# Attention probabilities transposed by DMA instead of by TensorE, with the exponentials left in PSUM

## What is computed

```
x = x + layernorm(attn(layernorm(x)))
x = x + layernorm(ffn(layernorm(x)))

attn(h): q, k, v = h@Wq, h@Wk, h@Wv          # rotary embedding on q and k
         p = softmax(where(causal, q@k^T, -1e9) / sqrt(64))
         return (p@v) @ Wo
ffn(h):  h @ weight^T + bias + lora(h)        # an adapter of rank 16 picked per batch
```

## Time and profile before

| | |
|---|---|
| Median of 3 runs | 2261.73 us |
| The profiled execution's own time | 2262.72 us |
| Its span, first to last instruction | 2260.9 us |
| PE busy | 2151.5 us, 95% of the span |
| DVE, ACT, POOL busy | 61%, 35%, 34% |
| Granted TensorE clock, mean | 0.978 |
| First slot of phase 1 starts, phase 2 starts | 98.44 us, 1516.18 us |

### The profile page before, as it was taken

The page is one execution under the profiler, slowest core; times in us unless marked ns, Lnnn a source line. Parts: engine busy times, 40 slices in busy tenths (PEclk is TensorE's granted clock), DMA queues, the critical chain, the costliest instruction groups (busy, mean ns, idle before and its releaser), DMA issues.

```text
span 2260.9 us, 35372 instructions
## 1 busy us (share of the span) xinstructions
PE 2151.5 (95%) x12928; PEld 1104.9 (49%) x12928; DVE 1386.0 (61%) x3295; ACT 791.6 (35%) x1797; POOL 773.7 (34%) x905
## 2 busy tenths in 40 slices
PE   3979999999999999999999998779999999999997
PEld 1445555555555555555555554444444444444443
DVE  6776566676576576566567565675555555555554
ACT  4544444444344444444444443532111111111111
POOL 0245455464554545455454544520000000000000
PEclk8999999999999999999999999979999999999999
DMA  7000010010010010010001020041433333423232
GB/s 294 1 29 15 20 43 11 24 34 19 24 31 24 10 43 24 10 44 20 15 29 33 15 85 10 20 177 47 121 94 84 97 82 97 117 64 114 62 79 56
DMA packets 98772, 125.47 MB, mean 55 GB/s; under 512 B 71745, under 2 KB 71745, under 8 KB 97570
## 3 DMA queue, kind: packets, MB, share of 16 engines
q1 hardware_dynamic: 98594, 123.12, 18.0%
HBM read 72.77 MB, written 33.55 MB: 47 GB/s over the span
## 4 chain that ended last, share of the span: by engine, by line
PE 90%; DVE 5%; issue 2%; POOL 1%; DMA 1%; ACT 1%; SPq 0%; POOLq 0%; DVEq 0%; ACTq 0%
PE ps L568 29%; PE ps L435 10%; PE ps L436 9%; PE ps L437 9%; PE ps L469 6%; PE ps L460 5%; PE ps L446 5%; PE ps L448 5%; PE ps L447 5%; PE ps L480 5%; PE ps L590 1%; PE ps L425 1%; POOL arena L1131 1%; DVE arena L711 1%; DVE w_part L620 1%
## 5 line engine op out<-in xcount | busy, mean ns | idle before, releaser
L1131 POOL TENSOR_TENSOR arena<-arena,row_inv 128x512 f32<-128x512 f32 (+3 forms) x512 | 357.9, 735 | 651.2 <-DVE row_inv L722 651.2
L435 PE MATMUL ps<-arena,region 128*128 128x512 f16 x1024 | 389.5, 380 | 0.0
L436 PE MATMUL ps<-arena,region 128*128 128x512 f16 x1024 | 388.9, 380 | 0.0
L437 PE MATMUL ps<-arena,region 128*128 128x512 f16 x1024 | 388.5, 379 | 0.0
L568 PE MATMUL ps<-region 128*128 128x512 f16 x1536 | 341.2, 383 | 8.5 <-ACT arena L1083 4.6
L807 DVE CUSTOM_DVE_ANT_0 arena<-ps,con,pow 128x512 f32<-128x512 f32 (+3 forms) x512 | 246.5, 547 | 162.1 <-PE ps L460 161.9
L568 PE MATMUL ps<-region,arena 128*128 128x512 f16 x1536 | 337.3, 379 | 0.0
L1050 ACT ACTIVATE arena<-arena,neg_max 128x512 f32<-128x512 f32 (+3 forms) x512 | 280.0, 548 | 99.3 <-DVE neg_max L807 99.3
L698 DVE TENSOR_TENSOR rotated<-ps,con 128x512 f32<-128x512 f32 x128 | 88.5, 691 | 266.7 <-PE ps L437 266.7
L568 PEld LDWEIGHTS ps<-region 128*128 128x128 f16 x1536 | 151.2, 99 | 193.5 <-issue 10.3
L1083 ACT ACTIVATE arena<-ps,sm 128x1024 f32<-128x1024 f32 x64 | 77.0, 1204 | 477.2 <-DVE sm L883 477.2
(11 more groups left out here) (121 smaller groups left out, 2668.2 us busy)
## 6 DMA issues: line engine op xcount, KB each, us to landing
arena<-x SPq DMA_DIRECT2D x32, 512.0 KB, 3.8
attn_scratch<-o_st SPq DMA_DIRECT2D x64, 256.0 KB, 2.2
region<-attn_scratch SPq DMA_DIRECT2D x8, 2048.0 KB, 8.8
v_split<-x SPq DMA_DIRECT2D x32, 512.0 KB, 4.2
out<-v_split SPq DMA_DIRECT2D x32, 512.0 KB, 5.1
arena<-wv SPq DMA_DIRECT2D x4, 1024.0 KB, 13.6
region<-wq SPq DMA_DIRECT2D x4, 1024.0 KB, 18.6
arena<-wk SPq DMA_DIRECT2D x4, 1024.0 KB, 5.5
```

The source lines that it names most:

```text
L435: mm(o, w[:, k, 0, cols], xnt[par][:, k, 0, :], start=(k == 0), stop=False)
L436: mm(o, w[:, k, 0, cols], xnt[par][:, k, 1, :], start=False, stop=False)
L437: last = mm(o, w[:, k, 1, cols], xnt[par][:, k, 0, :], start=False, stop=(k == KT - 1))
L1131: gp.tensor_tensor(unit_sb(j, a), unit_sb(j, a), row_inv[:, n:n + 1].broadcast_to([PART, 128 * (j + 1)]), ALU.mult).then_inc(norm_done, 1)
```

## The change

The scores stay in PSUM: DVE masks them in place and ACT takes the exponential in place. DVE takes all eight reciprocals at once and multiplies them by 2^14. ACT then writes the high part of the normalised probabilities (PSUM to SBUF, float16, scaled by a per-row factor) and DVE the low part, both as rows by query into `p_split`; POOL's `normalise` is gone. SP issues one transposing DMA of `p_split` (both parts, both heads: 128x5120 float16, 40 blocks of 128x128) into `pt`, after the low parts of the slot are done and the p@v products of the slot, which read the pair before from `pt`, are done. PE's `p_transposes` go. The p@v products read blocks of `pt` in 36 matmuls instead of 24, with the same number of columns, into bank 6, and wait for the DMA and for the first four low parts of the slot. Blocks of queries are now taken in the order 2, 0, 3, 1.

The normalised x of the next batch is split into two float16 tiles (ACT `xn_high_part`, DVE `xn_low_part`) and transposed by two DMAs of 128x1024, for batches 1 to 7; PE's `x_transposes` stay for batch 0 only. x comes in tile by tile into one buffer, each after the tile before is split.

As `p_split` and the x tile use the space in which Wo and Wf were staged, these come through two 1 MB buffers, and two chunks of each are loaded a second time for the split; two chunks of Wf after the last transposing DMA. `part_max` of Wo moves from slots 0 and 1 of the last batch to 1 and 2.

The diff, cut to its core:

```diff
-Q_ORDER = (3, 2, 0, 1)
-S_OFF = {3: 0, 2: 512, 0: 896, 1: 1024}
+Q_ORDER = (2, 0, 3, 1)
+S_OFF = {2: 0, 0: 384, 3: 512, 1: 1024}
 S_LEN = 1280
-UNITS = [(j, a) for j in Q_ORDER for a in range(2)]
+NB = S_LEN // PART
+UNITS = [(2, 0), (0, 0), (2, 1), (0, 1), (3, 0), (3, 1), (1, 0), (1, 1)]
 ...
+READY = (2, 2, 4, 4, 5, 6, 7, 8)
 ...
+PV_PIECES = {0: ((0, 2), (2, 2)), 1: ((1, 1), (2, 2)), 2: ((2, 2),), 3: ((3, 1),)}
+
+BANK_O = 6
 ...
+        raw_late = [arena2[:, at:at + 2048].rearrange("p (k n) -> p k n", k=KC) for at in (4096, 6144, 0, 2048)]
 ...
+
+        x_tile = arena2[:, 0:1024]
+        xn_high_t = arena2[:, 1024:1536].bitcast(F16)
 ...
-        scores = arena1[:, 4096:4096 + 2 * S_LEN].rearrange("p (a n) -> p a n", a=2)
-        pt = half(arena1[:, 6656:6656 + 2 * S_LEN], ("p (h g q) -> p h g q", dict(h=2, g=NG)))
+        pt = half(arena1[:, 6656:6656 + 2 * S_LEN], ("p (h n q) -> p h n q", dict(h=2, n=2 * NB)))
+        p_split = half(arena2[:, 1536:1536 + 2 * S_LEN], ("p (h a n) -> p h a n", dict(h=2, a=2)))
 ...
+                if not last_b and 1 <= p <= ST:
+                    tok = slice(128 * (p - 1), 128 * p)
+                    for hl, src in enumerate((xn_high_t, xn_low_t[:, :])):
+                        sp.wait_ge(xn_split[hl], n)
+                        if p == 1 and hl == 0 and not first:
+                            sp.wait_ge(qk_done[1], PAIRS * b)
+                        sp.nop(nofuse=True)
+                        sp.dma_start_transpose(xnt[1 - bp][:, :, hl, tok], src).then_inc(xnt_in[hl], 16)
                 if not last_b and p < ST:
 ...
+                    if first and p == 0:
+                        sp.wait_ge(xt_done, 2 * ST)
+                    else:
+                        need(sp, xn_split[1], n)
+                    sp.dma_start(x_tile, x_v[b + 1, p]).then_inc(x_next_in, 16)
+                if not (first and p == 0):
+                    sp.wait_ge(pv_done, g)
+                sp.wait_ge(p_done[1], 8 * g + 8)
+                sp.nop(nofuse=True)
+                sp.dma_start_transpose(pt[:, :, :, :].rearrange("p h n q -> p (h n) q"),
+                                       p_split[:, :, :, :].rearrange("p h a n -> p (h a n)")).then_inc(pt_in[0], 16)
 ...
+                if last_b and p == 0:
+
+                    for c in (0, 1):
+                        load_raw(W_O, c)
+                if last_b and p in (1, 6):
+                    w = {1: W_O, 6: W_F}[p]
+                    for c in (2, 3):
+
+                        sp.wait_ge(part_max_done, CHUNKS * {W_O: 1, W_F: 2}[w] + c - 1)
+                        load_raw(w, c)
+                if last_b and p == 4:
+                    for n in (0, 1):
+
+                        sp.wait_ge(w_low_done, CHUNKS * W_O + n + 1)
+                        load_raw(W_O, n, again=True)
+                if last_b and p == 5:
+                    for n in (0, 1):
+
+                        sp.wait_ge(w_low_done, CHUNKS * W_O + n + 3)
+                        load_raw(W_F, n)
+                if last_b and p == PAIRS - 1:
+                    phase2_loads()
 ...
+            sp.wait_ge(pt_in[0], 16 * PAIRS * B)
+            for c in (0, 1):
+                load_raw(W_F, c, again=True)
 ...
-            def p_transposes():
-                for bank, blocks in PT_GROUPS:
-                    for n, (a, kt, j) in enumerate(blocks):
-                        at = S_OFF[j] + 128 * kt
-                        last = nc.tensor.transpose(ps[:, bank, 128 * n:128 * n + 128], scores[:, a, at:at + 128],
-                                                   ident)
-                    last.then_inc(pt_done, 1)
-
 ...
-                        for a in range(2):
-                            grp, c = PT_ROW[kt][a]
-                            last = mm(ps[64 * a:64 * a + 64, BANK_O, 128 * kt:S],
-                                      v_split[:, kt, 2 * pair + a, HD * vl:HD * vl + HD], pt[:, hl, grp, c:c + n],
-                                      start=(kt == 0 and hl == 0 and vl == 0), stop=(kt == ST - 1 and hl == 1))
+                        for j, nq in PV_PIECES[kt]:
+                            at = S_OFF[j] // 128 + kt
+                            step = (S_OFF[j + 1] - S_OFF[j]) // 128 if nq == 2 else 1
+                            for a in range(2):
+                                blocks = pt[:, hl, NB * a + at:NB * a + at + (nq - 1) * step + 1:step, :]
+                                last = mm(ps[64 * a:64 * a + 64, BANK_O, 128 * j:128 * (j + nq)],
+                                          v_split[:, kt, 2 * pair + a, HD * vl:HD * vl + HD], blocks,
+                                          start=(kt == 0 and hl == 0 and vl == 0 and j == 0), stop=(kt == ST - 1 and hl == 1))
 ...
-                need(pe, pt_low, NG * g)
+                need(pe, p_done[1], 8 * g)
 ...
-                need(pe, masked, 8 * g + 8)
-                if not last_b and 1 <= p <= ST:
-                    need(pe, xn_done, 4 * b + 4 + p)
-                    for hh in range(2):
-                        x_transposes(p - 1, hh, BANK_XT[hh])
-                if has_qk:
                     need(pe, v_low, v_before(kind, p, b))
                     qk_product(1, n_pair, n_bp, range(KT), 1 - bank)
                 if not (first and p == 0):
+                    need(pe, p_done[1], 8 * g + 4)
                     need(pe, v_low, v_before(kind, p, b))
+                    need(pe, pt_in[0], 16 * g)
                     pv_products((p - 1) % PAIRS)
-                need(pe, norm_done, 8 * g + 8)
-                if not last_b and 1 <= p <= ST:
-                    need(pe, xt_low, 8 * b + 8 + 2 * p)
-                p_transposes()
                 if v_slot(kind, p):
 ...
-            def pt_evac(grp, n):
-
-                need(dve, pt_high, NG * n + grp + 1)
-                v.scalar_tensor_tensor(pt[:, 1, grp, :], ps[:, PT_GROUPS[grp][0], :], P_UP, pt[:, 0, grp, :],
-                                       ALU.mult, ALU.subtract).then_inc(pt_low, 1)
+            def p_low_part(g, n):
+
+                j, a = UNITS[n]
+                need(dve, p_done[0], 8 * g + READY[n])
+                v.scalar_tensor_tensor(unit_p(j, a, 1), unit_ps(j, a), row_inv[:, n:n + 1], unit_p(j, a, 0),
+                                       ALU.mult, ALU.subtract).then_inc(p_done[1], 1)
 ...
-            def inverse(g, part):
-
-                need(dve, exp_done, 8 * g + 4 * part + 4)
-                v.reciprocal(row_inv[:, 4 * part:4 * part + 4], row_sum[:, 4 * part:4 * part + 4]).then_inc(inv_done, 1)
+            def inverse(g):
+
+                need(dve, exp_done, 8 * g + 8)
+                v.reciprocal(row_rec[:, :], row_sum[:, :]).then_inc(recip_done, 1)
+                need(dve, recip_done, g + 1)
+                v.tensor_scalar(row_inv[:, :], row_rec[:, :], P_UP, None, ALU.mult).then_inc(inv_done, 1)
 ...
-                    if n in (0, 2, 6):
-                        need(dve, s_done, 3 * g + {0: 1, 2: 2, 6: 3}[n])
-                    if n == 0:
-                        need(dve, pt_done, NG * g)
+                    if n in (0, 4, 6):
+                        need(dve, s_done, 3 * g + {0: 1, 4: 2, 6: 3}[n])
                     v.nop(nofuse=True)
-                    v.tensor_tensor_reduce(out=unit_sb(j, a), in0=unit_ps(j, a), in1=causal[:, 512 - width:512],
+                    v.tensor_tensor_reduce(out=unit_ps(j, a), in0=unit_ps(j, a), in1=causal[:, 512 - width:512],
                                            scale=pow2[:, S_NEG:S_NEG + 1], scalar=HIGHEST, op0=ALU.add, op1=ALU.min,
                                            accum_out=neg_max[:, n:n + 1]).then_inc(masked, 1)
                 q = (p - 1) % PAIRS
                 if v_slot(kind if p > 0 else kind - 1, q) and not (first and p == 0):
 
                     v_evac(q % 4, 1 if q < 4 else 0, v_before(kind, p, b) - 1, 1 - bank)
-                inverse(g, 0)
+                if not last_b and 1 <= p <= ST:
+                    xn_low_part(4 * b + p - 1)
+                inverse(g)
                 if has_qk:
                     qk_drain(0, g + 1, bank)
-                inverse(g, 1)
-                if not last_b and p < ST:
-                    need(dve, x_in[p], 16 * (b + 2))
-                    ln_stats(p, 4 * b + 4 + p)
-                if not last_b and 1 <= p <= ST:
-                    for hh in range(2):
-                        xt_evac(p - 1, hh, 1 - bp, 8 * b + 8 + 2 * (p - 1) + hh, BANK_XT[hh])
-                if last_b and p < 2:
-                    part_max(W_O, 2 * p)
-                    part_max(W_O, 2 * p + 1)
+                need(dve, pt_in[0], 16 * g)
+                for n in range(len(UNITS)):
+                    p_low_part(g, n)
+                if last_b and p in (1, 2):
+                    part_max(W_O, 2 * (p - 1))
+                    part_max(W_O, 2 * (p - 1) + 1)
 ...
-                    qk_low_part(0, g + 1)
+                if not last_b and p < ST:
```

(78 more changed lines are left out.)

81 lines of the change are left out of this document (36 added, 45 removed), and 5 rows, old and new, of the table PT_GROUPS.

## The result

2133.1 us median (2129.9 to 2136.2, four runs) against 2261.7 (2261.2 to 2262.0, four runs): ratio 0.943, 95% interval 0.942 to 0.945. Forecast: 2127, range 2112 to 2172. The profiled execution took 2133.8 us, 6.0 more than the 2127.8 that the sum gave for it.

What follows compares the result with a forecast made beforehand. PE was taken to bound the slot wall to wall. Savings of 128.4 (batches 1 to 6) and 16.3 (batch 0), less 8.3 (batch 7) and 1.5 (second loads), took 2262.7 to 2127.8; median forecast 2127 us, range 2112 to 2172.

Steps and rivals of the forecast that it cites:

- PE bounds the slot, and the transposes cost it 2.24: Steady slots of phase 1: PE works wall to wall; dropping the probabilities' transposes shortens 21.47 us to 19.23.
- Twelve more p@v matmuls cost nothing: The p@v products of each slot: same columns in 36 matmuls; bounds 0 and 0.9 us a slot, 0 taken.
- The large DMA takes 8.2 us: Transposing DMA of each slot: 5 x 1.26 us issue plus 1.94 tail, hidden with 4 us to spare.
- Chain of k: Drain of k to its low part and the scores: 6.1 us, ready at 18.4 of 19.23, late next.
- Lows: DVE's low parts of the probabilities: 3.3 us, ending 11.65 into the slot, 0.65 us before the drain of k.
- Two turns of the loop, 0.9 us: Loop over batches 1 to 6: its two turns add 0.9 us to 48 slots of 19.23, making 923.9.
- Batch 0, 1.6 us for half clock: Slots 0.1 to 0.4: scores at half clock after idle add 1.6 us each; batch 156.9 us, 16.3 less.
- Batch 7, 8.3 us more: Last batch to phase 2's start: DVE's maxima and splits delay the drain of k; 200.6 us against 192.3.
- the gap ahead of the join: POOL in slot 7.2: first gap before the join of Wo counted in full; hidden, it would save 6 us.
- Rival 1: Chain around the large DMA sets the slot: above 19.23 past 14.4 us landing, gain gone from 17.6; total 2650; 5%.
- D: Time from issue to landing of each slot's large transposing DMA: taken as 8.2 us, between 3.2 and 16.
- The forms: Two formulas for the slot around the large DMA, landing after D us: D + 4 and (24.05 + D)/2.

Runs made afterwards that it cites:

- e6_dve_2p8: The changed kernel with one more DVE instruction of 2.8 us in each slot, between the low parts of the probabilities and the drain of k: 2239.3 us.
- e1_fifth: The changed kernel with the large transposing DMA cut to 8 of its 40 blocks in all slots but the first: 2123.4 us, ratio 0.939.
- e8_unrolled: The changed kernel with the loop over batches 1 to 6 written out: 2127.2 us, ratio 0.940.
- e9_best: The changed kernel with the last batch's extra DVE and POOL work reordered and, in slot 7.7, phase 2's first loads issued earlier: 2105.6 us, ratio 0.930.
- e10_best_unrolled: The changed kernel with the last batch reordered, phase 2's first loads earlier and the loop over batches 1 to 6 unrolled: 2097.1 us, ratio 0.927.

## Why the prediction was right, and where its terms were off

- *PE bounds the slot, and the transposes cost it 2.24:* right (slots of 19.25 after, 23.65 with twice the transposes). Twelve more p@v matmuls cost nothing: from the first of them to the V product 291.25 - 289.49 = 1.76 us, where 1.75 was measured with 24.
- *The large DMA takes 8.2 us, since its issue grows with size and its tail doesn't:* right to the first decimal (a tail of 2.2 us where 1.94 was taken, an issue of 6.03 where 6.3 was). The rule of the Trainium skill (page "VectorE: DVE Perf Modes", section "The three transpose paths") would make 52 us of it, an estimate; 8.2 us for 40 blocks is 0.2 us a block.
- *Chain of k late next, 0.8 us to spare:* right chain, spare 1.2 (e6_dve_2p8). Lows 0.44 longer than I took, and still ahead of the drain, by 0.2 where I had 0.65; the chain from the drain to the scores takes 5.8 and not my 6.1, POOL's two steps in it are shorter (means 1.27 and 1.28 us, 1.35 before).
- *Two turns of the loop, 0.9 us:* the term that failed most, 7.6. I took before's excess, in which no large DMA was under way. The text had asked what stands behind the DMA only for SP's own instructions, not for the engines' code, and had no half clock behind a turn (1.6 us in slot 3.0). With 0.02 us a slot this makes the +7.9.
- *Batch 0, 1.6 us for half clock:* mis-sized. I priced the scores alone; 2.2 us of the projections run at half clock as well, another 1.1 in each of slots 0.1 to 0.4. The trace of before had it: in its slot 0.1, after 6.16 us idle, the clock is 0.50 for 2.1 us behind the scores too (122.75 to 124.85). With 1.0 more in slot 0.0 (19.45, not 18.4; 18.70 in e1_fifth and e8_unrolled, where the clock stays up there) that is 5.4; the chain of k, faster than taken, gives back 0.6 in each of slots 0.1 to 0.3.
- *Batch 7, 8.3 us more:* 4.4. Slot 7.2 took 30.2 and not 35.4, as the gap ahead of the join was hidden, which the text had kept for the low end. The others are within 1.3 of their forecast.
- *Rival 1:* the first threshold, 14.4, is about right, the second, 17.6, too high: D = 14.7 already cost 45 us, and at about 16.2 the gain is gone. The forms left out late landings, the x DMAs in the same queue and the half clock behind waits. The D of this kernel, 8.2, is 6 below the first.
- *The sum of these* (-1.1 + 3.8 + 7.9 - 3.9 - 0.8 = 5.9) is the 6 us between forecast and profiled execution. The steady slots, 0.02 us off, are no luck. That the whole is off by 6 is in part: two terms took 11.7 too little, three took 5.8 too much.

## What to carry to other kernels

When one engine is busy wall to wall, the price of a piece of its work can be read off as a difference of two starts, and it holds until the next chain is late. So work out that chain's spare time to a few tenths. Then look at the slots that are not steady (first, last, loop turns), since the same edit costs there what it hides elsewhere: here they held 36 us beside the 129 gained, which another order of the last batch's work, earlier loads and an unrolled loop won. Ask of a large DMA what else is under way beside it, the engines' code included: here PE stood 2.7 us at a turn with a large one under way and 0.7 with a small one.

## What the runs showed of the hardware

- One transposing DMA of 40 blocks of 128x128 (2-byte) takes SP 6.03 us to issue and lands 8.2 us after its start; one of 8 blocks takes 1.23 and 3.0. Issue grows by 0.15 us a block ((6.03 - 1.23)/32), the tail behind it stays at 1.8 to 2.2.
- The same issue took 8.46 us (e9_best) and 6.63 (e10_best_unrolled) when 2 MB of plain loads had been issued ahead of it.
- At the two turns of the loop PE was idle for 2.69 and 2.87 us with such a DMA under way, 0.69 and 0.36 with one of a fifth of its size, 0.43 and 0.34 in the kernel before; with the loop unrolled there was no such gap.
- Exponentials in place in PSUM took a mean of 510 ns on ACT against 548 with SBUF tiles, masks in place 555 against 547 on DVE, which before went from PSUM to SBUF (the same mix of widths in each).
- A partition_all_reduce of 0.41 us left POOL idle for 7.16 us behind it.
- After 3.79 us without work PE ran the scores and 2.2 us of the projections at half clock (slot 0.2), 2.7 us more than in e1_fifth, where the same slot kept its clock after as long a wait (20.52 and 17.84).
